# Attention values for eight heads per PSUM bank, one 128x512 copy of each bank, and sixteen probability slots

## What is computed

```python
# self-attention: q, k get an RMS norm per head and rotary embedding; cross-attention: k, v come from ctx_1024
attn = einsum('bhqd,bhkd->bhqk', q, k) * scale
attn = softmax(where(causal, -inf, attn))
out  = einsum('bhqk,bhkd->bhqd', attn, v)
out  = out.transpose(0, 2, 1, 3).reshape(B, T, C) @ w_proj.T
# the layer
x = layernorm(x + self_attn(x));  x = layernorm(x + cross_attn(x, ctx, ctx));  x = layernorm(x + ffn(x))
```

## Time and profile before

| what | value |
|---|---|
| runs | 994.99, 996.09, 998.32 us; median 996.09 |
| profiled execution, first to last instruction | 995.1 us |
| PE busy | 907.2 us (91%), 7904 instructions |
| PE weight loads (PEld) busy | 709.5 us (71%) |
| DVE busy | 735.8 us (74%) |
| ACT busy | 496.2 us (50%) |
| POOL busy | 486.2 us (49%) |
| mean granted PE clock | 0.963 of full speed |

### The profile page before, as it was taken

One profiled execution on the slowest core, in us unless ns is written; L12 is line 12 of the kernel. 1 busy time (PEld: TensorE's weight loads), 2 busy tenths in 40 slices (PEclk: granted clock), 3 DMA queues, 4 the chain that ended last, 5 costly groups with the idle time before them and its releaser, 6 DMA issues.

```text
span 995.1 us, 21915 instructions
## 1 busy us (share of the span) xinstructions
PE 907.2 (91%) x7904; PEld 709.5 (71%) x7904; DVE 735.8 (74%) x1847; ACT 496.2 (50%) x1063; POOL 486.2 (49%) x899
## 2 busy tenths in 40 slices
PE   2467888999999999999999999999999999898896
PEld 2345565787878787787878787877878786777575
DVE  8777678677878878877778788888778787574612
ACT  1131443647465555646474655556464755455243
POOL 2173464545555564645464655646455546143221
PEclk9669899999999999999999999999999999999999
DMA  3909192836657290927566481909365563705000
GB/s 108 180 23 142 24 130 31 118 44 91 83 63 110 37 135 11 132 36 110 63 87 88 55 118 29 129 20 127 46 105 70 77 87 47 115 3 67 22 1 22
DMA packets 79644, 74.24 MB, mean 75 GB/s; under 512 B 8592, under 2 KB 78896, under 8 KB 79536
## 3 DMA queue, kind: packets, MB, share of 16 engines
q1 hardware_dynamic: 75872, 68.90, 49.9%
q10 hardware_dynamic: 3664, 3.94, 1.2%
HBM read 17.49 MB, written 4.20 MB: 22 GB/s over the span
## 4 chain that ended last, share of the span: by engine, by line
PE 56%; DVE 19%; issue 8%; POOL 5%; DMA 4%; SPq 3%; ACT 2%; POOLq 0%; ACTq 0%; DVEq 0%
PE bank L347 53%; DVE mx L899 8%; SPq L274 3%; POOL pr L1217 2%; DMA stk1k<-nat1k 2%; PE bank L372 2%; DVE x L980 2%; PE bank L571 2%; ACT pr L746 2%; DVE qn L1032 1%; DMA stk2q<-nat2q 1%; POOL rstd L1207 1%; DVE nat2q L882 1%; DVE nat2q L884 1%; DVE rest L875 1%
## 5 line engine op out<-in xcount | busy, mean ns | idle before, releaser
L746 ACT ACTIVATE pr<-bank 128x384 f32<-128x384 f32 x512 | 241.0, 501 | 192.4 <-PE bank L347 192.1
L899 DVE TENSOR_REDUCE mx<-bank 128x3 f32<-128x384 f32 x512 | 264.5, 551 | 82.5 <-PE bank L347 80.8
L1217 POOL TENSOR_SCALAR_AFFINE_SELECT pr<-pr 128x256 f32<-128x256 f32 x512 | 225.9, 453 | 183.1 <-ACT pr L746 179.9
L347 PE MATMUL bank<-cmaskb,idb 128*128 128x256 bf16 x512 | 145.2, 284 | 31.5 <-DVE mx L899 15.7
L347 PE MATMUL bank<-w,g 128*128 128x256 f32 x576 | 170.8, 389 | 1.1 <-ACT g L758 1.1
L758 ACT ACTIVATE g<-bank,b 128x256 f32<-128x256 f32 x144 | 68.4, 475 | 90.1 <-PE bank L347 89.8
L1241 POOL TENSOR_TENSOR xTlow<-xT,xThigh 128x512 fp32r<-128x512 f32 x16 | 21.2, 1324 | 161.1 <-ACT xThigh L682 161.1
L347 PEld LDWEIGHTS bank<-w,g 128*128 128x128 f32 x576 | 89.6, 190 | 5.2 <-ACT g L758 1.5
L347 PEld LDWEIGHTS bank<-cmaskb,idb 128*128 128x128 bf16 x512 | 50.3, 98 | 58.9 <-DVE mx L899 32.1
L347 PE MATMUL bank<-stk1k,stk1q 97*128 97x128 bf16 (+1 forms) x512 | 86.6, 258 | 0.0
L347 PE MATMUL bank<-stk1q,stk1k 100*128 100x256 bf16 (+1 forms) x512 | 80.0, 254 | 4.5 <-DMA stk1q<-mT 3.2
(11 more groups left out here) (157 smaller groups left out, 1829.3 us busy)
## 6 DMA issues: line engine op xcount, KB each, us to landing
stk1q<-nat1q SPq DMA_DIRECT2D x96, 128.0 KB, 4.6
stk1k<-nat1k SPq DMA_DIRECT2D x96, 128.0 KB, 6.5
stk2k<-nat2k SPq DMA_DIRECT2D x96, 128.0 KB, 4.7
stk2q<-nat2q SPq DMA_DIRECT2D x96, 128.0 KB, 6.1
xT<-in_xT SPq DMA_DIRECT2D x16, 256.0 KB, 7.2
ctxT<-in_ctxT SPq DMA_DIRECT2D x16, 256.0 KB, 7.8
x<-in_x SPq DMA_DIRECT2D x16, 256.0 KB, 6.1
out_x<-x SPq DMA_DIRECT2D x16, 256.0 KB, 5.9
```

The lines of the kernel that those rows point to most:

```text
L347: return nc.tensor.matmul(out, lhsT, rhs, start=start, stop=stop, skip_group_check=check)
L746: nc.scalar.activation(pr[:, h % (2 * HG), :], ring_bank("T", a, b, h)[:, 0:3 * P], ACT.Exp, scale=HD ** -0.5)\
L899: V.tensor_reduce(mx3[:, h, :], scored[:, 0:3 * P].rearrange("p (k t) -> p k t", k=3), AX.X, ALU.max, negate=True).then_inc(s_mx[a], 1)
L1217: G.affine_select(out=slot, in_=slot, compare_op=ALU.is_ge, fill=0.0, base=0, pattern=[[0, 2], [1, P]], channel_multiplier=-1).then_inc(s_ ...
```

## The change

`values` takes a pair of groups, eight heads: group 2p into columns 0 to 255 of bank 3 and group 2p + 1 into columns 256 to 511, sixteen products in a row. One `copy_pair` of 128x512 replaces two copies of 128x256. `pr` gets sixteen slots, one for each head, so a slot is reused an attention later. All counts of `s_pv` and `s_oT` are halved. In T1 and T2 `values` of pair 0 stands in front of head 11 and its copy ahead of exponential 14; `values` of pair 1 stays where group 3 stood (head 3 of the next phase). In T2, self-attention's last copy stands ahead of exponential 4 instead of 3. `pr` takes 12 KB more of each partition, and a scratch area for DMA descriptors is set to 1024 bytes.

```diff
-        pr = sb("pr", [P, 2 * HG, 3 * P])
+        pr = sb("pr", [P, H, 3 * P])
...
-            def values(a, b, gr):
-                pe.wait_ge(s_prob[a], H * b + HG * (gr + 1))
-                if gr == 0:
+            def values(a, b, pair):
+                pe.wait_ge(s_prob[a], H * b + PG * (pair + 1))
+                if pair == 0:
...
-                    pe.wait_ge(s_oT[a], NG * b + gr)
+                    pe.wait_ge(s_oT[a], NP * b + pair)
                 v = values_of(a, b)
...
+                for half in range(2):
+                    for key in range(2):
+                        for j in range(HG):
+                            h = PG * pair + HG * half + j
+                            out = bank[OT_BANK][VW * j:VW * (j + 1), half * T:(half + 1) * T]
+                            if key == 0:
+                                mm(out[:, 0:T], v[:, 0, h, :], pr[:, h, 0:T], True, False, True)
+                            else:
+                                last = mm(out[:, P:T], v[:, 1, h, :], pr[:, h, T:3 * P], False, True, True)
                 last.then_inc(s_pv[a], 1)
...
-                    for gr in range(NG - 1):
-                        add(HG * gr + VALUES_AFTER, values, 1, s, gr)
+                    for pair in range(NP - 1):
+                        add(PG * pair + VALUES_AFTER, values, 1, s, pair)
...
-                copy(oT[:, gr, :], bank[OT_BANK][:, 0:T]).then_inc(s_oT[a], 1)
+                copy(oT[:, 2 * pair:2 * pair + 2, :], bank[OT_BANK][:, :].rearrange("p (g t) -> p g t", g=2)).then_inc(s_oT[a], 1)
...
-                        if h % HG == 0 and h >= 2 * HG:
-                            copy_group(1, s, h // HG - 2)
+                        if h == COPY_PAIR_AT:
+                            copy_pair(1, s, 0)
                         exponential(1, s, h)
...
                         if h == COPY1_AT[0]:
-                            copy_group(1, s, NG - 2)
+                            high_part(2, s, 1, 0)
                         if h == COPY1_AT[1]:
-                            high_part(2, s, 1, 0)
+                            copy_pair(1, s, NP - 1)
                         if h == COPY1_AT[2]:
-                            copy_group(1, s, NG - 1)
-                        if h == COPY1_AT[3]:
                             copy_out(1, s)
...
-                        if h % HG == 0 and h >= 2 * HG:
-                            copy_group(2, c, h // HG - 2)
+                        if h == COPY_PAIR_AT:
+                            copy_pair(2, c, 0)
                         exponential(2, c, h)
...
-VALUES_AFTER = 7
+VALUES_AFTER = 11
...
-COPY1_AT, SQ_AT = (0, 3, 3, 9), (5, 10)
+COPY1_AT, COPY_PAIR_AT, SQ_AT = (3, 4, 9), 14, (5, 10)
...
-    nc = _bacc.Bacc("TRN2", target_bir_lowering=False, num_devices=1)
+    nc = _bacc.Bacc("TRN2", target_bir_lowering=False, num_devices=1, dynamic_dma_scratch_size=1024)
```

More of the change, by code:

```diff
@@ L57 @@
 NG = H // HG
+PG = 2 * HG
+NP = H // PG
 FCH = 9
@@ L449, in hidden @@
                     if live(b + 1):
-                        pe.wait_ge(s_oT[2], NG * (b + 2))
+                        pe.wait_ge(s_oT[2], NP * (b + 2))
                     else:
@@ L499, in transpose_max @@
                     if live(b - 2):
-                        pe.wait_ge(s_oT[2], NG * (b - 1))
-                    wait(pe, s_oT[1], NG * b)
+                        pe.wait_ge(s_oT[2], NP * (b - 1))
+                    wait(pe, s_oT[1], NP * b)
                 for t in range(TT):
@@ L523, in values @@
                     elif live(b + 1):
-                        pe.wait_ge(s_oT[1], NG * (b + 2))
+                        pe.wait_ge(s_oT[1], NP * (b + 2))
                     elif live(b - 2):
@@ L527, in values @@
                 else:
-                    pe.wait_ge(s_oT[a], NG * b + gr)
+                    pe.wait_ge(s_oT[a], NP * b + pair)
                 v = values_of(a, b)
[L530 to L537, removed]
+                for half in range(2):
[7 more added lines that the diff above has]
+                                last = mm(out[:, P:T], v[:, 1, h, :], pr[:, h, T:3 * P], False, True, True)
                 last.then_inc(s_pv[a], 1)
             def out_tokens(a, b):
-                pe.wait_ge(s_oT[a], NG * (b + 1))
+                pe.wait_ge(s_oT[a], NP * (b + 1))
                 for t in range(TT):
@@ L616, in step @@
                 if live(f):
-                    add(OUT2_AT[0], values, 2, f, NG - 1)
+                    add(OUT2_AT[0], values, 2, f, NP - 1)
                 if live(c):
@@ L656, in step @@
                     add(K2_AT, k2, s)
-                    add(OUT1_AT[0], values, 1, s, NG - 1)
+                    add(OUT1_AT[0], values, 1, s, NP - 1)
                 if live(i + 2):
@@ L669, in step @@
                 if live(c):
-                    for gr in range(NG - 1):
-                        add(HG * gr + VALUES_AFTER, values, 2, c, gr)
+                    for pair in range(NP - 1):
+                        add(PG * pair + VALUES_AFTER, values, 2, c, pair)
                 phase((lambda h: scores_t(2, c, h)) if live(c) else None, others)
@@ L685, in copy_v @@
                 act.wait_ge(s_v[a], b + 1)
-                wait(act, s_pv[a], NG * (b - 1) if a == 1 else NG * b)
+                wait(act, s_pv[a], NP * (b - 1) if a == 1 else NP * b)
                 copy(values_of(a, b)[:, :, :, 0:HD], bank[V_BANK[a]][:, :].rearrange("p (t h d) -> p t h d", t=TT, h=H))\
@@ L698, in copy_out, with copy_pair @@
                 copy_dims(onT[a], DIM_BANK[a]).then_inc(s_onT[a], 1)
-            def copy_group(a, b, gr):
-                act.wait_ge(s_pv[a], NG * b + gr + 1)
+            def copy_pair(a, b, pair):
+                act.wait_ge(s_pv[a], NP * b + pair + 1)
                 wait(act, s_ott[a], TT * b)
@@ L735, in exponential @@
                 act.wait_ge(s_st[a], H * b + h + 1)
[L737 to L741, removed]
+                if a == 1:
+                    wait(act, s_pv[2], NP * (b - 2) + h // PG + 1)
+                    wait(act, s_pv[1], NP * (b - 1) + h // PG + 1)
                 elif live(b + 1):
-                    act.wait_ge(s_pv[1], NG * (b + 1) + 3 + h // HG)
+                    act.wait_ge(s_pv[1], NP * (b + 1) + h // PG + 1)
                 else:
-                    act.wait_ge(s_pv[2], NG * (b - 1) + 3 + h // HG)
-                nc.scalar.activation(pr[:, h % (2 * HG), :], ring_bank("T", a, b, h)[:, 0:3 * P], ACT.Exp, scale=HD ** -0.5)\
+                    act.wait_ge(s_pv[2], NP * (b - 1) + h // PG + 1)
+                nc.scalar.activation(pr[:, h, :], ring_bank("T", a, b, h)[:, 0:3 * P], ACT.Exp, scale=HD ** -0.5)\
                     .then_inc(s_exp[a], 1)
@@ L778, in step @@
                 if live(f):
-                    copy_group(2, f, NG - 1)
+                    copy_pair(2, f, NP - 1)
                 if live(c):
```

4 lines of the change are left out of this document (1 added, 3 removed).

## The result

The changed kernel takes 1030.23 us (median of 4 runs, 1027.77 to 1033.3) where the kernel before takes 997.21 us beside it (median of 4, 994.99 to 1000.57). The ratio is 1.0325, with a 95% interval of 1.0302 to 1.0348: slower. The profiled execution has a span of 1030.8 us against 995.1 us, 35.7 us more. The forecast was 1021 us; its range of 1000 to 1034 us holds the result, and the forecast itself is 9 us short. The profiled run of the changed kernel took 1032.55 us, 2.3 us above the median of the four.

The account below looks back on a forecast made before the run. PE's list of work was taken to bound the middle, busy 54.40 of 55.05 us a step. Terms summed to +1.62 us in eleven steps plus +7.2 us at the ends, +25 us: 1021 us, range 1000 to 1034 us.

Parts of the forecast that it names:

- the vanishing ring: Rival: exponentials keep ahead, three ring terms (1.53 us a step) vanish; +0.09 us a step, about 1000 us; chance 0.13.
- the switching halves: Rival: a pair's halves switch like two groups, so the 0.80 us is not saved; 1031 us; chance 0.10.
- switches: four pairs for eight groups: PE, values: each pair saves one 128x32 entry and exit, 0.20 us; four pairs a step, -0.80 us.
- T1 to T2, ring: PE, T1's head 15 and T2's head 0 wait for exponentials 12 and 13: net +0.47 us a step.
- `out_tokens`: T2: waits for self-attention's copy behind exponential 3, no longer covered by `qk1`; 1.42 us instead of 0.18, +1.24 a step.
- behind `out_tokens`: T2: heads 7 and 8 wait for exponentials, `out_dims` for `on`: +0.67 us a step.
- T2 to S1: S1's head 0 waits for exponential 13; heads 1, 2 and values lose time too: net +0.39 us a step.
- DVE's waits come back: S1: DVE stands about 1 us further ahead, so PE's waits for it shrink: -0.35 us a step.
- The ring: Three score banks: head h waits for exponential h - 3, so four heads in a row on PE wait.
- The ends: Steps 0 to 2, 14, 15 and drain: together +7.2 us, with 2.2 each for steps 1 and 2, drain 0.9.
- The clock rival: Rival: the new wait brings the low clock in each step, some 22 us more, 1043 us; chance 0.08.
- The faster rival: Rival: copy released at head 3, covered by `qk1`, no ring; -0.80 us in 13 steps, about 986 us; chance 0.05.

Follow-up runs that it names:

- experiments 1: Changed kernel with self-attention's last copy ahead of T2's exponential 3 again instead of 4: 1012.29 us, ratio 1.0155.
- experiment 2: Kernel before, without pairs, with self-attention's last 128x256 copy ahead of T2's exponential 4 instead of 3: 1011.06 us, ratio 1.0148.
- Experiment 5: Changed kernel with groups at their old places, two sharing a bank, one 128x512 copy for both, last copy ahead of exponential 3: 1001.33 us, ratio 1.0044.
- Experiment 4: Changed kernel with POOL's power `rr` ahead of T1's mask 8 instead of mask 5: 1018.11 us, ratio 1.0221.
- Experiment 9: Kernel with pairs for self-attention only, its copy, `rr` and `ffn_out` moved, plus `transpose_xn` at T1's head 13 instead of 12: 990.84 us, ratio 0.9936.
- experiment 10: Changed kernel with copy, `rr`, `v1`, `squares` and one `ffn_out` moved, plus `transpose_x1` at S1's head 2, `transpose_xn` at T1's head 13: 994.04 us, ratio 0.9974.
- experiment 8: Control: kernel before, no pairs, with `rr` ahead of mask 8 and the last `ffn_out` at T1's head 14: 999.81 us, ratio 1.0017.
- experiments 6: Changed kernel with cross-attention back in four groups, copy ahead of exponential 3, `rr` ahead of mask 8, one `ffn_out` at T1's head 14: 994.86 us, ratio 0.9973.

## Why the prediction was right, and where it fell short

The sign, the mechanism and the four places of the loss that it names were right. The size was 10.7 us short on the profiled execution (35.7 us against 25). The distances between `transpose_x1` of the two profiled executions divide it: steps 3 to 13 grew by 21.9 us (forecast 17.8), everything else by 13.8 us (forecast 7.2). One term of the middle and the clock of the ends are missing in the forecast; the sum still fell inside the stated range because that was made wide for other cases, the vanishing ring and the switching halves. The narrower range of the forecast by itself, 1010 to 1030 us, ends just under the measured time.

**A middle step, term by term** (starts on PE, after less before):

| Term | forecast us | measured us |
|---|---|---|
| switches: four pairs for eight groups | -0.80 | -0.92 |
| T1, head 6 to pair 0: mask of POOL | none | +0.35 |
| T1 to T2, ring | +0.47 | +0.56 |
| `out_tokens` | +1.24 | +1.23 |
| behind `out_tokens` | +0.67 | +0.73 |
| T2 to S1 | +0.39 | +0.41 |
| DVE's waits come back | -0.35 | -0.37 |
| sum | +1.62 | +1.99 |

- **Switches.** The second half of a pair follows at the pace within a group: 1.44 us a pair, forecast 1.47, and 1.67 had the halves switched. The rival with switching halves falls. It had 1031 us, almost the measured time, so the total alone would have spoken for the wrong cause; the pair's row decides. The Trainium skill (TensorEngine Tiling (Array Packing), Key Properties) says that changing the tiling mode drains TensorE and changing the tile does not; the trace agrees, with 1.44 us a pair.
- **`out_tokens`.** +1.23 us, forecast 1.24. The prediction took ACT's queue as in order, and experiments 1 and 2 show it from both sides. Its 0.07 us for the release stands in no row; here it is 0.05 us (530.95 + 0.59 to 531.59). The advice of the Trainium skill (Perfetto Trace Analysis, Optimizing Scalar/DVE Operations) to break instructions up where they make bubbles elsewhere would have brought an estimated 0.2 us here, by the narrow copy of experiment 2 (0.86 against 1.07 us of wait); two copies in the shared bank were not run. Moving the undivided copy by one place in the queue brought all of it.
- **The ring.** Two of the three places came within 0.1 us, and the third within 0.02 us. (The parts of the first, 0.43 and 0.20 less 0.18 us, add up to 0.45 and not to the 0.47 that the prediction has.) The rival in which these terms vanish falls: 0.85 us a step is waited for exponentials alone, besides what is lost at these places otherwise. Experiment 5 shows the cause: with groups at their old places no head waits.
- **The missing term.** The prediction said "masks are done about when PE comes to the values" for T2 and did not ask it for T1's pair 0. There group 0 no longer stands ahead of head 7, so PE comes 0.88 us earlier, while POOL still computes `rr` for 0.70 us between masks 4 and 5 and then needs 0.59 and 0.85 us for masks 6 and 7. The prediction had masks at 0.40 us throughout. From head 6 to pair 0, 2.41 us were to be expected (3.29 before, from 499.65 to the row below, less 0.88) and 2.76 are there (518.90 to 521.66). Experiment 4 takes it away: -0.38 us. Over eleven steps this is 3.9 of the 4.1 us by which the middle fell short. PE's row of group 1 in the kernel before:

```profile
502.94 0.86 PE L347 MATMUL bank<-pr,va1a 128*32 128x256 f32 x16
```

- **The ends.** Steps 1 and 2 cost 3.9 and 4.7 us instead of 2.2 each, the drain 3.8 instead of 0.9; steps 14 and 15 together 1.0 where 1.2 was forecast. The terms had waits, switches and the longer pair in them, and the clock in step 14 alone. In steps 1 and 2 and the drain together PE's busy time grew by 9.0 us (161.7 to 170.7) of the 12.4 us, and the granted clock fell from 0.86 to 0.82, from 0.94 to 0.88 and from 0.95 to 0.90. What is left for waits is 3.4 us, less than the 5.3 us forecast there. So the term that failed is one that was left out again: the clock at the ends. Steps 1 and 2 before, then in the changed kernel (the rows of the drain stand in experiment 4):

```profile
88.70:138.50 49.80, 43.94 (x368) 30.14 (x365) 34.74 (x82) 21.36 (x50) 26.45 (x51) 0.86 0.60 80
138.50:191.80 53.30, 45.51 (x404) 32.44 (x404) 40.65 (x105) 23.45 (x56) 28.54 (x54) 0.94 0.58 76
```

```profile
89.10:142.80 53.70, 45.73 (x351) 30.75 (x349) 34.77 (x82) 20.42 (x46) 26.09 (x50) 0.82 0.57 77
142.80:200.80 58.00, 48.60 (x404) 33.99 (x404) 40.80 (x105) 22.95 (x52) 28.14 (x54) 0.88 0.54 70
```

PE's timeline of step 2 in the changed kernel shows it in the pair that stands behind the masks, and the busy time of that stretch has the clock, 0.50, the 1.2 GHz level:

```profile
177.52 2.79 PE L349 MATMUL bank<-pr,va1a 128*32 128x256 f32 x32 [1.53 <-POOL pr L1214]
```

```profile
177.50:180.50 3.00, 2.98 (x34) 1.59 (x35) 2.24 (x5) 0.00 (x0) 1.15 (x3) 0.50 0.02 5
```

- **The clock rival** falls for the steps it was made for: with 1.07 us of wait a step the granted clock stays 1.00 in the middle. What it describes happens at the ends, where the prediction had not looked.
- **The faster rival** named the right condition: the copy released at head 3, covered by `qk1`, and no ring. Experiment 9 fulfils it by other edits, experiment 10 but for 0.26 us a step of the ring, and both come out faster.

What stays open: why the clock of the ends differs between these kernels, as the last section shows; and whether the kernel before would gain from `transpose_xn` at head 13 along with the two moves of experiment 8, which was not run. By the `xn` waits of that control (0.31 us a step of its 55.33) it would come to 55.02, the step of the kernel before, and all of kernel 9's 0.33 us would be due to the pairs. But that move brought 0.38 us in kernel 9 where the wait was 0.24 us, so the control may come out lower. What runs show of the pairs at like places is the 0.25 us a step between experiments 6 and 8; the rest of kernel 9's gain is open.

## What to carry to other kernels

Work that is merged leaves empty places, and a merge is priced by what the moved pieces were covering: list, for each old place, which consumer on which engine then comes earlier, and what that consumer waits for, on every engine and not only on the one that is saved. Where a copy that the bottleneck waits for stands in an in-order queue, ask first what stands ahead of it; one place in ACT's queue was worth 1.2 us a step here, half the copy's width 0.2 us. And a saving is only cashed when the next chain (here DVE's `x` and `xn`) is given the same time.

## What the runs showed of the hardware

- A wait of 1.07 us on PE in each step of 57 us left the granted clock at 1.00.
- The length of the one wait ahead doesn't tell the clock behind it. The last pair of the drain waited 1.78 us for a mask in the changed kernel and 1.77 us in kernel 4, at the same place of the program; then it took 2.58 us in the one and 1.51 us in the other (granted clock 0.56 over 981.5:984 and 1.00 over 971.5:980). And step 2's pair took 2.77 us in kernel 4 too, without a wait right in front of it. PE's timelines of the changed kernel (one row) and of kernel 4 (three):

```profile
981.51 2.58 PE L349 MATMUL bank<-pr,va 128*32 128x256 f32 x32 [1.78 <-POOL pr L1214]
```

```profile
172.90 1.10 PE L349 MATMUL bank<-stk1q,stk1k 100*128 100x256 bf16 x6 [0.25 <-ACT pr L747]
174.13 2.77 PE L349 MATMUL bank<-pr,va1a 128*32 128x256 f32 x32
...
971.58 1.51 PE L349 MATMUL bank<-pr,va 128*32 128x256 f32 x32 [1.77 <-POOL pr L1214]
```

- Steps 1 and 2 and the drain, a fifth of the time, thus carry several microseconds that no term of waits gives: 4.1 us of busy time in the drain alone, for the same 520 matmuls at a clock of 0.90 instead of 0.94.
- Values into the second half of a bank follow the first without a gap: 1.44 us for 32 PE instructions in the 128x32 form, 0.79 us for 16.
- Masks of one shape did not take one time on POOL: 0.41 us mostly, but 0.59 and 0.85 us for two of them beside work of DVE.
